# The first group of heads in another order: first tile ahead, eight PSUM banks as two sets of four, transposes and splits moved; unit 0 of the experts and the last scatter re-ordered

## The reference, cut to what matters

```python
# xattn: per batch row, 32 heads of 8 rows, 512 positions; h = head
kv  = einsum('bhil,bhjl->bijhl', k_, v_)          # k = v = ctx: 8 x 8 products, 36 distinct
y   = causal convolution of kv with ssm_kernel[h] # + kv * D[h]
out = einsum('bijhl,bhil->bjhl', y + kv*D, q_)    # q = layernorm(x)
x   = x + out
# ffn: t = layernorm(x), softmax router, top 4 of 16 experts, at most 256 tokens each
y   = sum over chosen experts of w * (silu(t @ w_gate[e]) * (t @ w_up[e])) @ w_down[e]
out = x + y + (silu(t @ sw_gate) * (t @ sw_up)) @ sw_down
```

## Time and profile before

| what | value |
|---|---|
| median of 3 runs (lowest to highest) | 614.12 us (614.03 to 621.5) |
| profiled execution | 613.82 us, of it span 612.0 us |
| TensorE busy | 590.2 us, 96% of the span |
| VectorE busy | 485.7 us, 79% |
| GpSimd busy | 408.1 us, 67% |
| ScalarE busy | 289.8 us, 47% |
| chain that ended last | TensorE 78%, VectorE 8% |

### The profile page before, as it was taken

How to read it: one execution, slowest core, us unless ns; L and a number is a source line. 1 busy time by engine, 2 the same in 40 slices (tenths; PEclk the granted TensorE clock), 3 DMA queues, 4 the chain that set the end, 5 groups by cost and what they waited for, 6 DMA issues and landing times.

```text
span 612.0 us, 13711 instructions
## 1 busy us (share of the span) xinstructions
PE 590.2 (96%) x4411; PEld 551.9 (90%) x4411; DVE 485.7 (79%) x1279; ACT 289.8 (47%) x520; POOL 408.1 (67%) x500
## 2 busy tenths in 40 slices
PE   7979999999999999999999999899999999999993
PEld 6758989999999989999999898899999999999992
DVE  6999787679789689598799889989888888887730
ACT  3426334434435334344351344576655666656731
POOL 6998799778888789789771372187788833334342
PEclk9999999999999999999999999999999999999997
DMA  6665315225336145241230247788878888888543
GB/s 180 230 185 172 104 36 172 78 76 160 87 94 171 43 114 152 62 136 43 86 112 2 58 154 245 245 232 225 235 214 225 229 227 241 237 233 244 136 56 48
DMA packets 60238, 91.50 MB, mean 150 GB/s; under 512 B 4262, under 2 KB 36006, under 8 KB 60188
## 3 DMA queue, kind: packets, MB, share of 16 engines
q1 hardware_dynamic: 52912, 74.00, 39.8%
q0 software_dynamic: 7168, 16.78, 13.5%
q10 hardware_dynamic: 108, 0.08, 0.1%
HBM read 73.76 MB, written 17.09 MB: 148 GB/s over the span
## 4 chain that ended last, share of the span: by engine, by line
PE 78%; DVE 8%; issue 4%; POOL 3%; ACT 2%; DMA 2%; DVEq 1%; POOLq 0%; SPq 0%; ACTq 0%
PE gu L684 19%; PE gu L843 14%; PE yb L562 11%; PE mb L860 10%; PE gu L722 7%; PE yb L843 7%; PE mb L534 4%; PE yb L614 3%; PE yb L534 2%; POOL kv L1251 1%; DVE prod L1515 1%; DVE prod L1517 1%; DVE oT L1535 1%; DVE ew L1811 1%; PE yb L814 1%
## 5 line engine op out<-in xcount | busy, mean ns | idle before, releaser
L684 PE MATMUL gu<-xT,sw 128*128 128x256 f32 (+2 forms) x1104 | 136.4, 281 | 0.0
L684 PEld LDWEIGHTS gu<-xT,sw 128*128 128x128 f32 (+2 forms) x1104 | 131.9, 180 | 0.5 <-issue 0.2
L1251 POOL TENSOR_TENSOR kv<-kT 128x256 f32 (+3 forms) x232 | 106.4, 499 | 0.0
L1268 POOL TENSOR_TENSOR kvl<-kv,kvh 128x1440 fp32r<-128x1440 f32 (+1 forms) x26 | 82.4, 3168 | 26.1 <-ACT kvh L970 25.8
L1515 DVE TENSOR_TENSOR prod<-yb,qT 128x64 f32<-128x64 f32 (+10 forms) x272 | 73.9, 282 | 17.3 <-PE yb L614 11.7
L1535 DVE TENSOR_REDUCE oT<-prod 128x256 f32<-128x2048 f32 x32 | 72.8, 2276 | 0.1
L970 ACT ACTIVATE kvh<-kv 128x1440 fp32r<-128x1440 f32 (+1 forms) x26 | 35.2, 1352 | 74.4 <-POOL kv L1258 37.5
L562 PE MATMUL yb<-kvh,tlast 128*128 128x288 f32 x280 | 66.1, 297 | 0.0
L1517 DVE TENSOR_TENSOR prod<-yb,qT 128x96 f32<-128x96 f32 (+10 forms) x238 | 63.2, 266 | 0.0
L860 PE MATMUL mb<-ed,midh 128*128 128x512 f32 x180 | 57.4, 400 | 0.0
L1811 DVE TENSOR_TENSOR ew<-raw_w,ew 128x704 fp32r<-128x704 f32 x64 | 55.1, 881 | 0.3 <-ACT ew L1118 0.3
(11 more groups left out here) (218 smaller groups left out, 1293.8 us busy)
## 6 DMA issues: line engine op xcount, KB each, us to landing
raw_w<-in_L_ffn_w_gate_dram SPq DMA_DIRECT2D x16, 704.0 KB
raw_w<-in_L_ffn_w_up_dram SPq DMA_DIRECT2D x16, 704.0 KB
raw_d<-in_L_ffn_w_down_dram SPq DMA_DIRECT2D x16, 512.0 KB, 4.3
tlast<-toeplitz_taps SPq DMA_DIRECT2D x20, 384.0 KB, 3.6
tstep<-tap_steps SPq DMA_DIRECT2D x20, 256.0 KB, 4.1
c_t<-in_ctx_dram SPq DMA_DIRECT2D x16, 256.0 KB, 5.2
x_t<-in_x_dram SPq DMA_DIRECT2D x16, 256.0 KB, 5.3
normalised_tokens<-xn SPq DMA_DIRECT2D x16, 256.0 KB, 2.9
```

The costliest lines, as they stand in the source:

```text
L684: last = pe.matmul(bank[0:m, u * GT:(u + 1) * GT], sw[:, c, a, col:col + m], xT[:, c, b, :], start=(c == 0 and (a, b) == PASSES[0]), stop= ...
L1251: last = pool.tensor_tensor(to[:, :, POFF[d]:POFF[d] + w], src[:, :, 0:w], src[:, :, d * B:HD * B], ALU.mult)
L1268: pool.tensor_tensor(kvl[:, s, 0:nb, :], kv[:, s, 0:nb, :], kvh[:, s, 0:nb, :].bitcast(fp32), ALU.subtract)\
```

## The change

All of it stands in the start, the first group, the first group's post-work, expert units 0 and 1, and the last expert. No product of the computation is added or left out (five sixths of the idle products on the identity go: 8 instead of 22).

- **PSUM.** `gu` and `mb` become the halves of one tensor `other` of four banks. Heads 0, 2 and 4 convolve into `yb`, 1 and 3 into `other`, each in one piece; `BY_HALVES` is (0, GH, GH+1), with GH = 4. The post-work of group 0 transposes into `gu` (`turned`) instead of `mb`.
- **Start.** The taps are loaded and written first, by SP; x comes tile by tile, tile 0 by ScalarE's queue. Statistics, power, normalising and transposes of tile 0 are done before those of tile 1 (`first_stats`, `inverse_tile`). FIRST_POOL is 4: VectorE makes four of head 0's eight products, GpSimd four. The gate rows are transposed before head 0, and head 1 waits for `gate_l`. Tile 1's queries are transposed before the last block of head 2, behind `d_mul` 2, which is VectorE's multiply of head 1.
- **Steps of the taps.** `steps_of` is rounded by ScalarE and its remainder taken by GpSimd, between the splits, instead of both by VectorE at the start.
- **Later in group 0.** On TensorE head 4 is convolved in one piece, then wait for `d_mul` 4, `prep_q(1)`, `mixed_out` of tile 0, the first half of head 5, `mixed_out` of tile 1, `normalised`, the second half of head 5; `prep_ctx(2)` comes behind the two `gate_up` instead of ahead of them. On GpSimd `inverse_t(0)` and the splits of pieces 0, 2, 1 and 3 are moved.
- **Experts.** In unit 0 VectorE and ScalarE do the rows and the last weight piece of expert 1 ahead of the second middle; VectorE also does the third middle and `one_hot(3)` in unit 0 instead of unit 1. In `last_down` two passes and one pass of `part(0, 1)` are moved around the wait; the last expert's scatter has no memset of `carrier`.

Three places of the order, as each engine's program has it.

The diff, cut to its core:

```diff
-        BY_HALVES = (0, 1, 2, GH, GH + 1)
-        FIRST_POOL = 3
+        BY_HALVES = (0, GH, GH + 1)
+        FIRST_POOL = 4
...
-        FIRST_HOMES = {1: ((gu, 0), (yb, 0)), 2: ((yb, 2), (gu, 0)), GH: ((gu, 0), (yb, 0)),
-                       GH + 1: ((yb, 2), (yb, 0))}
+        FIRST_HOMES = {1: ((other, 0), (other, 2)), 3: ((other, 0), (other, 2)), GH + 1: ((mb, 0), (yb, 0))}
+
+        def turned(g):
+            return gu if isinstance(g, int) and g == 0 else mb
...
+            sp.dma_start(tap_rows[:], taps).then_inc(taps_in, 16)
+            sp.dma_start(c_t[:, 0, :], c_g[0, 0]).then_inc(ctx_first[0], 16)
+            sp.wait_ge(pad_whole, 1)
+            sp.dma_start(first_dram, pad[0:WHOLE, :]).then_inc(first_out, 16)
+            sp.dma_start(c_t[:, 1, :], c_g[0, 1]).then_inc(ctx_first[1], 16)
             sp.wait_ge(first_out, 16)
             load_first(0)
+            sp.dma_start(x_t[:, 0, 1, :], x_g[0, 1]).then_inc(x_first[1], 16)
+            load_first(1)
+            load_first(2)
+            sp.wait_ge(c_tr, TT)
+            load_group(1, parts="c")
+            load_first(3)
             load_group(1, parts="x")
-            load_first(1)
             sp.wait_ge(taps_hl, 1)
             sp.dma_start(toep_dram, padhl[:].bitcast(fp32)).then_inc(taps_out, 16)
-            sp.wait_ge(c_tr, TT)
-            load_group(1, parts="c")
             load_shared(0)
-            load_first(2)
-            load_first(3)
             load_shared(1)
             load_shared(2)
-            sp.wait_ge(steps_hl, 1)
-            sp.dma_start(step_dram, stephl[:].rearrange("n h d c -> n (h d) c").bitcast(fp32)).then_inc(steps_out, 16)
...
+                    if n == 1 and half == 0:
+                        pe.wait_ge(gate_l, 1)
                     if n == 1 and half == 1:
-                        pe.wait_ge(d_half, 1)
+                        pe.wait_ge(k_ev, TT)
+                        pe.wait_ge(q_ev, 1)
                     if n == 2:
-                        pe.wait_ge(*((d_mul, 1), (d_half, 2))[half])
+                        pe.wait_ge(d_mul, 1)
                     if n == 3:
-                        pe.wait_ge(*((d_mul, 2), (d_half, 3))[half])
+                        pe.wait_ge(*((d_mul, 2), (k_ev, 2 * TT))[half])
                     if n == GH:
-                        pe.wait_ge(d_mul, (3, 4)[half])
+                        pe.wait_ge(d_mul, 3)
                     if n == GH + 1:
-                        pe.wait_ge(*((d_mul, 4), (d_half, 4))[half])
+                        pe.wait_ge(*((q_ev, 2 * TT), (d_half, 2))[half])
...
+                    convolve(GH * g, 0)
+                    pe.wait_ge(d_mul, 4)
+                    prep_q(g)
+                    mixed_out(g - 1, g, [0])
+
+                    def turn():
+                        mixed_out(g - 1, g, [1])
+                        normalised(g - 1)
+
+                    convolve(GH * g + 1, 1, turn)
+                if prep and chunk:
                     prep_ctx(g + 1)
                 if post:
                     gate_up(g - 1, 0)
                     gate_up(g - 1, 1)
+                if prep and not chunk:
...
-            prep_ctx(0)
-            idle_products(17)
-            convolve(0, 0, {1: lambda: prep_q(0)})
+            gate_turned()
+            prep_ctx(0, [1])
+            idle_products(1)
+            prep_q(0, [0])
+            convolve(0, 0)
+            convolve(1, 1)
+
+            def second_queries():
+                pe.wait_ge(d_mul, 2)
+                prep_q(0, [1])
+
+            convolve(2, 2, {LB - 1: second_queries})
...
-            evacuate(kT, 0, c_tr, k_ev, c_tr, 0)
-            norm_q(0)
-            evacuate(qT, 0, q_tr, q_ev, q_tr, 0)
+            evacuate(kT, 0, c_tr, k_ev, c_tr, 0, [0])
+            norm_q(0, [0])
+            act.wait_ge(gate_t, 1)
+            act.activation(sw[:, :, 0, IS:UP], gu[:, 1, 0:LB * E].rearrange("p (c e) -> p c e", c=LB),
+                           ACT.Copy).then_inc(gate_h, 1)
+            evacuate(qT, 0, q_tr, q_ev, q_tr, 0, [0])
+            evacuate(kT, 0, c_tr, k_ev, c_tr, 0, [1])
+            norm_q(0, [1])
+            evacuate(qT, 0, q_tr, q_ev, q_tr, 0, [1])
+            split_shared(0)
             evacuate(kT, 1, c_tr, k_ev, kv_m, 0)
-            split_shared(0)
-            act.wait_ge(gate_t, 1)
-            act.activation(sw[:, :, 0, IS:UP], mb[:, 0, 0:LB * E].rearrange("p (c e) -> p c e", c=LB),
-                           ACT.Copy).then_inc(gate_h, 1)
+            act.wait_ge(steps_ok, 1)
+            act.activation(stephl[:, 0, :, :], steps_of[:], ACT.Copy).then_inc(steps_h, 1)
             split_shared(1)
             split_shared(2)
             norm_q(1)
+            split_shared(3)
...
+                if before:
+                    e_round(e, k, 1)
+                    round_rows(e + 1, 1 - k)
+                else:
+                    round_rows(e + 1, 1 - k)
+                    e_round(e, k, 1)
+                    e_silu(e, k, 2)
...
+            inverse_tile(1, x_stat, x_pow, x_rs)
             pairs(2, 0, 2)
             pairs(3, 0, 3)
+            split_shared(0)
+            pool.wait_ge(steps_h, 1)
+            pool.tensor_tensor(stephl[:, 1, :, :], steps_of[:], stephl[:, 0, :, :].bitcast(fp32), ALU.subtract)\
+                .then_inc(steps_hl, 1)
+            inverse_x(1)
             pairs(GH, 1, 0)
-            inverse_x(1)
+            split_shared(2)
             pairs(GH + 1, 1, 1)
-            split_shared(0)
-            split_shared(2)
+            inverse_t(0)
             split_shared(1)
...
+            def meanwhile():
+                first_stats(1, x_stat)
+                gate_low()
+
+            multiply(0, 0, 0, meanwhile)
...
+                    low_rows(e + 1, 1 - k)
+                    low_w(e + 1, 1 - k, 3)
+                else:
+                    low_rows(e + 1, 1 - k)
+                    low_w(e + 1, 1 - k, 3)
+                    e_middle(e, k, 1)
+                    one_hot(e + 3)
                 e_low(e, k, 1)
+                if not before:
+                    e_middle(e, k, 2)
                 low_d(e, k)
+                if not before:
+                    e_low(e, k, 2)
```

More of the change, by code:

```diff
@@ L867, in last_down, with part @@
                 pe.wait_ge(ed_l, e + 1)
[L869 to L870 removed]
+                def part(j, h, passes=PASSES):
+                    for a, b in passes:
                         last = pe.matmul(mb[:, h, :], (midh, midl)[a][0:EK[j], EJ * k + j, h * P:(h + 1) * P],
@@ L954, in norm_tokens, with evacuate @@
                          trs, tnb, t_nrm)
-            def evacuate(dst, g, arrived, signal, free, free_at):
-                for t in range(TT):
+            def evacuate(dst, g, arrived, signal, free, free_at, tiles=range(TT)):
+                for t in tiles:
                     act.wait_ge(arrived, TT * g + t + 1)
```

180 lines of the change are left out of this document (95 added, 85 removed).

## The result

The changed kernel took 623.57 us (median of 4 runs, 622.1 to 624.18) against 614.08 for the kernel before beside it: ratio 1.013, interval 1.0085 to 1.0176. (The quotient of the medians would be 1.0155; the ratio also takes in a run of the kernel before at 621.5.) On another chip, beside experiments 6 to 8, it took 621.3 (7 runs, 620.07 to 623.46), ratio 1.0106 (1.0068 to 1.0144). The forecast of 617.0 and its range up to 619.8 were both too low. The profiled execution took 622.1, its span is 620.1.

A forecast was written before the change was run, and what follows sets the result against it. Three queues (TensorE, VectorE, GpSimd) bound the program's head; after the change GpSimd ends last, starting head 6 4.8 us later. Sum: 613.8 + 4.8 - 1.3 (expert unit 0) - 0.3 (last scatter) = 617.0 us, range 612.2 to 619.8.

The forecast's parts named there:

- the waits: First group: TensorE waiting for head 4's pairs until 36 to 38; GpSimd idle some 3 us, then some 4.
- `trs`: GpSimd's inverse of the tokens in the first group: expected at 47 to 49 us; before 45 would mean wrong.
- head 6: TensorE in the first group: expected to wait for `kvl` until 62 to 64 us; before 59 would mean wrong.
- second rival: TensorE's clock falls in heads 0 or 4, some 4 us at the lower level: 2.0 us lost, 619.0, chance 0.20.
- Start at 11.3, gain 0.7: Program start: head 0 starts at 11.3 us instead of 12.0, bounded by the taps; bounds 10.4 and 12.0.
- The chain over the queries, ScalarE's copy and the first split to head 4's pairs: First group: GpSimd waits 3.2 us for the split; head 4's pairs end at 36.8, TensorE waits 3.2 us.
- Head 4 36.8 to 41.8: TensorE, first group: head 4's ten products run from 36.8 to 41.8, some 5.0 us.
- GpSimd behind `t_stat`, 15.1 us: First group: GpSimd needs 15.1 us from `t_stat` at 47.9 to head 6's `kvl` at 63.0; head 6 4.8 later.
- GpSimd's next remainders have some 1 to 2 us to spare by the same prices: Behind head 6: what follows moves with it, and GpSimd's next remainders have some 1 to 2 us to spare.
- Expert unit 0, 1.3: TensorE's 1.55 us wait for the last `ew` remainder shrinks with the rows issued earlier: gain 1.3, bounds 0 and 1.55.
- The last scatter, 0.3: End of the kernel: without the memset the last scatter's DMA starts earlier, gain 0.3, between 0.1 and 0.44.
- Whole multiplies and steps off VectorE: VectorE, first group: whole multiplies of heads 1 and 2 save 0.8 us each, 1.7 in all; steps worth nothing.

The follow-up runs named there:

- experiments 6 to 8: Changed kernel, ScalarE's rounding and first split earlier; GpSimd's piece 1, pieces 1 and 3, or piece 1 (plus 28 TensorE fillers) earlier: 614.39, 616.52, 613.5 us.
- Experiment 2: Changed kernel with ScalarE's rounding of the steps and first weight split ahead of the copy of tile 1's queries: 616.75 us, ratio 1.0024.
- experiment 3: Changed kernel with GpSimd's remainders of weight pieces 1 and 3 ahead of `inverse_t(0)`: 620.49 us, ratio 1.0088.
- experiment 4: Kernel before with only the change's expert part and the last scatter without its memset: 612.97 us, ratio 0.9979.
- experiment 6: Changed kernel with ScalarE's rounding and first split ahead of tile 1's query copy, and GpSimd's piece 1 ahead of `inverse_t(0)`: 614.39 us, ratio 0.9987.

## Why the prediction was wrong, point by point

Of the signs that the prediction named, the waits stand where it has them; `trs` (50.15, not 47 to 49) and head 6 (65.25, not 62 to 64) are later, and the sign of its second rival, a granted clock below 1 in the first 60 us, is there.

- **Start at 11.3, gain 0.7: too small.** Head 0 started at 10.34. The read back was issued 1.66 us after the write, where the rows of before had 3.28. Runs differ here: head 0 started between 10.3 and 11.0 in the eleven traces with this start, so the forecast was 0.3 to 1.0 us late, and the lower bound (10.4) was the better choice.
- **The chain over the queries, ScalarE's copy and the first split to head 4's pairs: right.** GpSimd idle 3.53 (3.2 forecast), steps 1.28 (1.2), TensorE's wait 3.42 (3.2). Experiment 2 removes it with three instructions and head 4 starts without it.
- **"Head 4 36.8 to 41.8": this step failed.** It prices ten products at full clock (5.0) behind a wait of 3.2 us, and they took 8.12. The clock was a rival of its own with a chance of 0.20 and 2.0 us, against 0.50 for a sum without it; it came true, and in this execution cost more. Counted from head 0's start, so that its spread drops out, head 6 comes after 54.9 us in the changed kernel (65.25 - 10.34) and after 52.0 with both waits filled (63.00 - 10.98): the clock costs 2.9. The 2.0 was half of "some 4 us at the lower level"; head 4's products ran 6.1 us at it. In experiment 3's trace they lost 1.8, so the price was right for one execution and too low for the other; what was wrong in both is a sum that puts the clock at nothing. The argument for the low chance was that the trace of before "has no such wait in mid-kernel", which is a reason for not knowing, not one against. The Trainium skill ("TensorE: Matmul & The Clock Gate", Part 1) says that an idle engine falls to half the clock and needs sustained work to leave it. The trace agrees at both long waits, 3.42 and 4.24 us: a granted clock of 0.50 came with each. The rival's other place, head 0, came to nothing: with 8 of 22 idle products left (fourteen go, not the five sixths that the section on the change says) head 0 ran in 5.02 us.
- **GpSimd behind `t_stat`, 15.1 us: right** (15.0), and so was the name of the bound: `kvl` ends at 65.15 and head 6 starts at 65.25. Experiment 3 shows that TensorE with its two waits was as late, where the forecast had it 2.1 us earlier.
- **"GpSimd's next remainders have some 1 to 2 us to spare by the same prices": this step failed too.** There is nothing to spare. From the start of head 6's `kvl` to the end of the fifth `midl` GpSimd needs 62.50 to 92.69, 30.2 us with 2.2 idle, and TensorE is back 28.7 us after the start of `kvl`. The stall is 1.75. One price that was missing is that of the pairs of head 9: 5.33, not 3.5. It could have been read in the trace of before (5.38). With 3.5 the stall would be gone (30.2 - 1.8 = 28.4, against 28.7), but 1 to 2 us to spare would not be there either; how the forecast came to them its text does not say.

  The kernel before gives the slack itself. There head 6's `kvl` started 7.2 us ahead of head 6 (51.02 to 58.25), and GpSimd was idle for 4.5 us up to the fifth `midl`. Of these 2.0 are a wait for ScalarE that stands in both traces; the other 2.5 are what lateness could use up. The forecast itself takes 4.6 us off the lead (the `kvl` that was ready 4.6 ahead of head 6 is now what head 6 waits for), so a stall of some 2 us could have been worked out.

  The Trainium skill ("SBUF — State Buffer", "SBUF: two separate sides") says that GpSimd and a VectorE instruction with two SBUF inputs share a port pair and that one blocks the other. The trace agrees in kind: 1.8 us are added to GpSimd's pairs beside VectorE's four subtractions, and these take 1.84 and 2.02 us a pair here and 1.55 and 1.60 in the kernel before, so both sides are lengthened. How much of VectorE's time is its own waiting no run shows, and none moves the subtractions away.
- **Expert unit 0, 1.3: right**, 1.4 in experiment 4 and 1.5 in the changed kernel.
- **The last scatter, 0.3: nothing.** Its bounds began at 0.1. The 0.64 ahead of the DMA was read as a time that starts at the memset's end; it is part of 0.84 that start at ScalarE's end.
- **Whole multiplies and steps off VectorE: not shown by themselves.** No run undoes them. In experiment 6 they are in, and the head is no faster than before (58.44 against 58.25), so whatever they save on VectorE is not on the path there.

The sum with the measured terms is 617.0 - 1.0 (start, in this execution) + 3.1 (head 4) + 1.75 (down) + 0.3 (scatter) - 0.2 (experts) + 1.1 (0.3 between head 6 and the down product, 0.5 behind the last scatter, 0.2 outside the span, 0.1 rounding) = 622.05, and 622.1 was profiled. The median of 623.57 lies 1.5 above this execution. With both waits filled four of five runs lay within 0.6 us, with the first alone filled eight of nine within 0.5, while the unaltered kernel's seven spread over 3.4. Of these seven the three with a mean granted clock of 0.985 took 621.7 to 623.5 and the four with 0.988 to 0.990 took 620.1 to 621.3; but of the first four runs the one with the lowest clock is the fastest. That the clock makes the spread is likely, and not shown.

## What to carry to other kernels

A wait of TensorE such as the 3.4 us here has two prices: its own length, and the slower clock of the work behind it, here 3.1 us on 5.0 and in another execution 1.8; put both into the sum, and give the second the better chance where the wait itself is forecast. When work is moved on one engine's queue, walk that queue to the place where it last had slack, with the duration that each instruction has there and not the one that it has elsewhere; of its idle time up to there only the part that shrinks when the queue comes late is slack. A filler must be no longer than the wait, and in a trace it earns nothing where another engine sets the end.
